# A perceiver block on one core: the dense softmax moved to the head of the following step

## The chip, the core and the metric

The kernel runs on one core of a Trainium2 chip. Its engines are TensorE (PE: matrix products and transposes, into PSUM), VectorE (DVE), ScalarE (ACT), GpSimd (POOL) and SyncE (SP, which only issues transfers); each runs its own list of instructions in order, and they wait for one another through semaphores. Sixteen DMA engines move data between HBM and the on-chip memory SBUF; SP and ACT issue to them. The metric is the device time of one execution in microseconds (us), lower is better, as the median of several executions.

## The reference

Sixteen sequences of 64 queries (width 512) attend to 16 long sequences of 1601 keys (width 384). Three blocks follow one another, each on a layer norm of the running x, and each adds to x:

```python
x = x + cross_attention(layernorm(x), ctx)   # one head of 512: softmax(q k / sqrt(512)) v, then Wo
x = x + attention(layernorm(x))              # 16 heads of 32, 64 positions; clip(q k / sqrt(32)) + q . rel[i - j],
                                             # softmax, divided once more by (its sum + 1e-8), then Wo
x = x + ffn(layernorm(x))                    # gelu(x W1 + b1) W2 + b2 with W1, W2 rounded to -1, 0, 1 by a threshold
```

## The kernel before, in words

Two sequences make a pair, 128 rows of x, so there are 8 pairs (tiles). A step n works on three of them at once: pair p = n in the cross attention, tile t = n - 1 in the first half of the dense attention, tile r = n - 2 in what is left of it. Steps 0 to 7 run; then the last two tiles finish, and the feed-forward part runs over 32 hidden blocks (2 halves of x by 16 blocks of 128 hidden units). Each engine's list is written out by hand in its own `step(n)`; all waits are semaphores.

Cross attention of pair p. PE turns the inverse deviations of the keys into rows (`key_factors`, L756), DVE multiplies the raw scores with them and finds the maximum (`scale_scores`, L1204; `exp_bias`, L1210 to 1215), ACT takes exponents in three parts (`exps`, L530), PE turns them by groups (`turn_probs`, L858), DVE scales them (`pt_scale`, L1222), and PE multiplies them with the keys as they lie (`weighted`, L871). ACT scales the context (`context_scale`, L536), PE turns it (`turn_context`, L903), and after `cT_out` (L541) `xattn_o` (L916) makes the output. DVE adds it to x and takes the moments (`x1_sum`, L1285), POOL makes the inverse deviation (`row_rstd`, L399), DVE normalises (`x1_norm`, L1294), PE turns the result (`y_turn`, L952). In the same step the next pair is prepared: statistics of its keys on DVE (`key_stats`, L1166), a power on POOL (`rstd`, L394), its x turned (`x_turn`, L723), the row that meets the keys (`a_rows`, L733), an offset (`key_offsets` on POOL, L381; `key_offset_sums` on ACT, L508), and the raw scores in four chunks (`scores`, L780) in the order 0, 1, tail, 2. The key tiles come twice: as they lie (`load_nat`, L265) and turned (`load_kt`, L278), the turned chunks through two buffers.

Dense attention of tile t. `q_rows` (L791), which opens PE's step, and `k_rows` (L802); `relative` (L833) for the relative part. A row of the relative part has to be shifted by its position: ACT copies it to SBUF (`g_out`, L567), stores it to HBM (`skew_store`, L572) and loads it back with a slanted pattern (`skew_load`, L580). `att_scores` (L844) and `clip` (DVE, L1237) make the other part, POOL adds the two (`radd`, L405), DVE subtracts the row maximum (`row_shift`, L1243 and L1245), ACT takes exponents (`row_exp`, L585), DVE makes the factors (`row_scale`, L1250 to 1260), POOL multiplies (`probs_scale`, L410), PE turns the probabilities (`att_turn`, L944). All of that is in step n = t + 1. In the next step come `att_values` (L816), `ctx_out` (L560), `att_o` (L896), `x2_sum` (L1302), `x2_norm` (L1310) and `z_turn` (L928); `values` and `v_out` (L885, L1268) make the values of tile t.

What sets the order around the change is each engine's hand-written list. POOL's in a step: x_norm, x_bias, radd(t), row_rstd(r), add_fb2(r), rstd(p+1, first half), key_offsets, probs_scale(t), rstd(p+1, second half), row_rstd(p), add_abo(p). DVE runs the statistics of the next pair's seven key groups in between: clip(t) after group 0, x2_sum(r) after 1, x2_norm(r) after 2, row_shift(t) and v_out(t) after 3, row_scale(t) after 4, and x1_sum, z_low, x1_norm after 6. The weights' magnitudes for the rounding are summed on ACT in steps 1 to 6 (`magnitude`, L608), six a step, each with a load of its own on SP.

Feed-forward. From step 7 on POOL compares the weights with the lower threshold (`neg`, L429) and DVE makes -1, 0, 1 (`ternary`, L1347). For hidden block i: PE `hidden` (L1088), ACT `gelu` (L703), DVE the high half (`gh`, L1441) and the low half (`gl`, L1443) in fp16, PE `ffn_out` (L1103) two blocks later. The softmax of the last tile is put in between at fixed blocks.

At the start PE makes a product of the two cross weights (L711), and in step 0 a product of the values' weights (`value_product`, L990), their mean (`value_mean`, L999, then `value_center` on DVE, L1363) and a bias row (`value_bias`, L1006).

Of the kernel before, what the change touches and what calls it, by code (L numbers as in the profile page):

```python
# [11 lines left out]
P = 128  # L12
# [4 lines left out]
def build_program(nc, A, out):  # L17
# [25 lines left out]
    with ctx:  # L43
# [71 lines left out]
        yTx, at = carve(at, [P, KD, P])  # L115
        a_sb, at = carve(at, [P, KC, P])
        cT, at = carve(at, [P, KC, P])
        cnat, at = carve(at, [P, DC])
# [6 lines left out]
        ssb, _ = carve(GS_AT, [P, H, L])  # L125
        psb = ssb
        b1row, _ = carve(GS_AT, [P, D])
# [27 lines left out]
        at += (NT - 2) * 4 * KD * P  # L155
        pT = []
        for _ in range(2):
            v, at = carve(at, [P, 4, P])
            pT.append(v)
# [33 lines left out]
        def sm(a, n=1):  # L193
# [9 lines left out]
                 "rel_loaded dense_loaded abv_loaded kt_tail_loaded skew_stored skew_loaded stored").split()  # L203
# [40 lines left out]

        def group(g):

            return (4, P) if g < 3 else (1, TAIL)
# [10 lines left out]
        def _(sp):  # L258
# [10 lines left out]
            def load_kt(p, ch):  # L269
# [5 lines left out]
                i = NCH * p + ch  # L275
                if i >= 2:
                    sp.wait_ge(s["chunk_scored"], 4 * ((i - 2) // NCH) + PLACE[(i - 2) % NCH] + 1)
# [31 lines left out]
            load_kt(0, NCH)  # L309
            sp.dma_start(wvT, A["wvT"]).then_inc(s["wvo_loaded"], 16)  # L310
            sp.dma_start(wo, A["wo"]).then_inc(s["wvo_loaded"], 16)
            load_kt(0, 2)
# [3 lines left out]
            load_kt(1, 0)  # L316
            load_kt(1, NCH)
            load_kt(1, 1)
# [6 lines left out]
            def step(n):  # L325
                wms, following = magnitudes(n), magnitudes(n + 1)
                more = n + 1 < NT
                for k in range(NG + 1):
# [4 lines left out]
                if n == 0:  # L333
                    sp.wait_ge(s["vbias_ps"], 1)
                    for i in range(1, 4):
                        sp.dma_start(aw[i], A["aw"][i]).then_inc(s["dense_loaded"], 16)
                if n + 2 < NT:
                    load_x(n + 2)
                if more:
                    load_kt(n + 1, 2)  # L340
                if len(wms) > 5:
                    load_wm(wms[5])
                if n + 2 < NT:
                    load_kt(n + 2, 0)
                    load_kt(n + 2, NCH)
                    load_kt(n + 2, 1)
# [14 lines left out]
        def _(pool):  # L361
# [74 lines left out]
            def step(n):  # L436
                p, t, r = stages(n)
                more = p + 1 < NT
                if more:
                    x_norm(p + 1)  # L440
                    if n == 0:
# [3 lines left out]
                        x_bias(0)  # L445
                    x_bias(p + 1)
# [3 lines left out]
                if t is not None:  # L450
                    radd(t)
# [9 lines left out]
                if t is not None:  # L461
                    probs_scale(t)
                if more:
                    rstd(p + 1, 1)
                row_rstd(p, "ln1_var", "ln1_rstd", VE1, RS1)
                add_abo(p)

# [3 lines left out]
            neg(6)  # L471
            row_rstd(LAST_T - 1, "ln2_var", "ln2_rstd", VE2, RS2)
            add_fb2(LAST_T - 1)
            neg(7)
# [10 lines left out]
        def _(act):  # L485
# [70 lines left out]
            def ctx_out(r):  # L556

                act.wait_ge(s["values_ps"], r + 1)
                for o, src in enumerate((W[1], U)):
                    act.copy(ctxT.rearrange("p (c o) r -> p o c r", o=2)[:, o, :, :], src[:, 0:2 * P].rearrange("p (c r) -> p c r", r=P)).then_inc(s["values_taken"], 1)  # L560

            def g_out(t):

                act.wait_ge(s["relative_ps"], t + 1)
                at_least(act, s["probs_turned"], 2 * t)
# [21 lines left out]
            def probs_out(t):  # L587

                at_least(act, s["values_ps"], t)
                for i, src in enumerate((W[0], W[1]) if t < LAST_T else (W[1], U)):  # L590
# [35 lines left out]
            def step(n):  # L626
                p, t, r = stages(n)
                wms = magnitudes(n)
                more = p + 1 < NT
                exps(p)  # L630
                if n == 0:
                    for m in range(KC):
                        act.wait_ge(s["xvo_ps"], m + 1)
                        act.copy(xwvo[:, m, :], S[m]).then_inc(s["xvo_taken"], 1)
                if t is not None:
                    q_out(t)
# [3 lines left out]
                if r is not None:  # L640
                    ctx_out(r)
                for i in wms[0:2]:
                    magnitude(i)
                if t is not None:
                    skew_load(t)
                context_scale(p)
                if more:
                    yTx_out(p + 1)
                if n == 0:
                    act.wait_ge(s["vbias_ps"], 1)  # L650
# [878 lines left out]
```

## Time and profile before

| | us |
|---|---|
| median of 3 runs | 689.96 |
| lowest, highest | 682.02, 702.35 |
| the profiled execution | 693.69 |
| its span, first to last instruction | 692.0 |
| PE, DVE, POOL, ACT busy in it | 556.3, 343.2, 202.1, 189.9 |

The profile is of one execution on the chip. Times in its rows count from the span's start. An engine name with q is its queue of issues; "granted clock" is the share of full speed at which TensorE's clock was let through; "idle before" is the time in which the engine stood before the instruction, with what released it. In shapes and names, `area` is the one large SBUF tensor that holds all buffers, `s_ps`, `u_ps` and `w_ps` are PSUM.

### The profile page before, as it was taken

What the parts mean: (1) busy time and instruction counts of PE and PEld (TensorE: products, weight loads), DVE (VectorE), ACT (ScalarE), POOL (GpSimd) and SP (SyncE); (2) the same over time, 40 slices, a digit from 0 to 9 for tenths busy, and PEclk for the clock granted to TensorE, in tenths of its full rate; (3) what the DMA queues carried; (4) which work ended last, traced back from release to release, by engine and by line L of the source; (5) the groups of instructions that cost most, each with busy time, mean ns of one, the idle gap of its engine ahead of it and who ended that gap; (6) DMA issues with size and microseconds to landing.
All of it is one profiled execution on the core that took longest, in us unless ns stands there. A gap on an engine that the chain in (4) does not pass through costs nothing.

```text
span 692.0 us, 10456 instructions
## 1 busy us (share of the span) xinstructions
PE 556.3 (80%) x4171; PEld 318.4 (46%) x4171; DVE 343.2 (50%) x769; ACT 189.9 (27%) x447; POOL 202.1 (29%) x136
## 2 busy tenths in 40 slices
PE   3979989907894989589678949896892878899997
PEld 1834455505452745365254517453641733344443
DVE  5814644453267237435732582284348178955333
ACT  0232124122413422341224124322401323121111
POOL 0131242042225204320522251043347376710000
PEclk9889999967998899799989988997996899999999
DMA  8975995925485387449544953760432242001001
GB/s 320 391 295 202 349 371 200 325 74 198 144 300 210 123 262 265 139 169 340 166 185 143 309 209 122 218 238 31 169 91 91 93 92 91 31 1 53 9 1 62
DMA packets 41617, 122.46 MB, mean 177 GB/s; under 512 B 19544, under 2 KB 21336, under 8 KB 36704
## 3 DMA queue, kind: packets, MB, share of 16 engines
q1 hardware_dynamic: 23776, 109.20, 43.5%
q10 hardware_dynamic: 17792, 12.58, 7.1%
q8 instruction: 33, 0.54, 0.3%
q14 instruction: 16, 0.13, 0.1%
HBM read 111.29 MB, written 10.49 MB: 176 GB/s over the span
## 4 chain that ended last, share of the span: by engine, by line
PE 42%; DMA 20%; DVE 12%; POOL 12%; ACT 7%; issue 6%; ACTq 1%; SPq 0%; DVEq 0%; POOLq 0%
DMA area<-skew 13%; PE s_ps L1103 7%; PE w_ps L1088 6%; PE s_ps L780 5%; PE u_ps L791 4%; PE u_ps L871 4%; POOL area L394 4%; DVE area L1166 4%; DMA skew<-area 3%; POOL area L429 3%; ACT area L567 2%; POOL area L405 2%; DMA area<-in_kt_dram 2%; PE s_ps L711 2%; PE w_ps L896 2%
## 5 line engine op out<-in xcount | busy, mean ns | idle before, releaser
L1166 DVE BATCH_NORM_STATS2 area<-area 128x6 f32<-128x384 f32 (+1 forms) x208 | 99.3, 544 | 3.9 <-DMA area<-in_nat_dram 3.9
L780 PE MATMUL s_ps<-area 128*64 128x512 f32 (+1 forms) x384 | 79.5, 560 | 5.8 <-DMA area<-in_kt_dram 4.7
L871 PE MATMUL u_ps<-area 128*64 128x384 f32 (+1 forms) x416 | 81.9, 543 | 0.3 <-DVE area L1222 0.3
L1103 PE MATMUL s_ps<-area 128*128 128x512 f16 x256 | 61.0, 381 | 8.6 <-DVE area L1443 8.6
L952 PE MATMUL w_ps<-area 128*128 128x128 f32 x32 | 8.5, 415 | 72.5 <-DVE area L1294 72.5
L1222 DVE TENSOR_TENSOR area<-w_ps,area 128x512 f32<-128x512 f32 (+1 forms) x32 | 18.8, 591 | 90.3 <-PE w_ps L858 90.3
L429 POOL TENSOR_SCALAR area<-area 128x512 f16<-128x512 f32 x32 | 54.9, 1730 | 28.1 <-DVE area L1334 14.3
L1088 PE MATMUL w_ps<-area 128*128 128x512 f16 x256 | 61.7, 383 | 0.1
L405 POOL TENSOR_TENSOR area<-area 128x1024 f32<-128x1024 f32 x8 | 18.8, 2354 | 145.6 <-DMA area<-skew 145.6
L1204 DVE CUSTOM_DVE_ANT_0 area<-w_ps,area 128x512 f32<-128x512 f32 x24 | 15.3, 689 | 89.6 <-PE w_ps L756 89.6
L780 PEld LDWEIGHTS s_ps<-area 128*64 128x64 f32 x384 | 25.9, 150 | 51.2 <-issue 48.9
L871 PEld LDWEIGHTS u_ps<-area 128*64 128x64 f32 (+1 forms) x416 | 30.6, 150 | 38.9 <-issue 37.3
L703 ACT ACTIVATE area<-w_ps,area 128x512 f32<-128x512 f32 x32 | 21.9, 687 | 88.8 <-PE w_ps L1088 74.3
L394 POOL TENSOR_TENSOR area<-area 128x16 f32<-128x16 f32 (+1 forms) x16 | 39.0, 2440 | 17.5 <-DVE area L1181 17.5
L1103 PEld LDWEIGHTS s_ps<-area 128*128 128x128 f16 x256 | 24.4, 97 | 40.6 <-DVE area L1443 10.8
L952 PEld LDWEIGHTS w_ps<-area 128*128 128x128 f32 x32 | 5.4, 207 | 73.7 <-DVE area L1294 73.7
L1088 PEld LDWEIGHTS w_ps<-area 128*128 128x128 f16 x256 | 24.6, 97 | 31.8 <-issue 3.0
L1441 DVE TENSOR_SCALAR area<-area 128x512 f16<-128x512 f32 x32 | 17.5, 547 | 43.3 <-ACT area L703 43.3
L1347 DVE SCALAR_TENSOR_TENSOR area<-area 128x512 f16<-128x512 f32 x32 | 31.1, 1014 | 14.4 <-POOL area L429 11.2
L371 POOL TENSOR_TENSOR area<-area 128x1 f32<-128x1 f32 x8 | 4.9, 610 | 112.4 <-DVE area L1154 112.4
L896 PE MATMUL w_ps<-area 128*128 128x512 f32 x64 | 31.1, 629 | 2.4 <-ACT area L560 2.4
L791 PEld LDWEIGHTS u_ps<-area 128*128 128x128 f32 x256 | 30.3, 197 | 5.7 <-issue 5.7
(167 smaller groups left out, 901.7 us busy)
## 6 DMA issues: line engine op xcount, KB each, us to landing
area<-in_nat_dram SPq DMA_DIRECT2D x48, 768.0 KB, 9.8
area<-in_kt_dram SPq DMA_DIRECT2D x24, 1536.0 KB, 6.7
area<-in_wf_dram SPq DMA_DIRECT2D x32, 256.0 KB, 7.2
skew<-area ACTq DMA_DIRECT2D x8, 1024.0 KB, 3.9
area<-in_wf_dram SPq DMA_DIRECT2D x16, 512.0 KB, 3.3
area<-in_aw_dram SPq DMA_DIRECT2D x4, 1024.0 KB, 7.8
area<-skew ACTq DMA_DIRECT2D x16, 256.0 KB, 6.8
area<-in_x_dram SPq DMA_DIRECT2D x8, 256.0 KB, 10.4
```

The costliest lines, as they stand in the source:

```text
L394: pool.tensor_tensor(rs[p % 2][:, sl], ve[:, sl], minus_half[:, 0:sl.stop - sl.start], ALU.pow).then_inc(s["rs_ready"], 1)
L405: pool.tensor_tensor(ssb, ssb, rsk, ALU.add).then_inc(s["radd_done"], 1)
L429: pool.tensor_scalar(wneg[f % 2][:, w, :], wraw[f % 4][:, w, :], sm(WNTHR + w), None, ALU.is_lt).then_inc(s["neg_done"], 1)
L703: act.activation(gf[i % 2], HID[i % 2][:, :], ACT.Gelu, bias=col("ffn_b1", i % KF), scale=1.0).then_inc(s["gelu_done"], 1)
L780: ins = pe.matmul(S[ch][u * L:(u + 1) * L, 0:n], a_sb[:, c, u * L:(u + 1) * L], x[:, u, c, :], start=(c == 0), stop=(c == KC - 1))
L791: ins = pe.matmul(U[:, m * P:(m + 1) * P], awq[:, c, m * P:(m + 1) * P], yT[:, c, :], start=(c == 0), stop=(c == KD - 1))
L871: ins = pe.matmul(U[u * L:(u + 1) * L, 0:DC], pT[g % 2][0:m, i, u * L:(u + 1) * L], nat[0:m, j, u, :], start=(j == 0), stop=(j == NJ - 1))
L896: ins = pe.matmul(dst[:, :], ctxT[:, c, :], awo[:, c, :], start=(c == 0), stop=(c == KD - 1))
L1088: ins = pe.matmul(HID[i % 2][:, :], wf16[:, f, 0, c * P:(c + 1) * P], zt[:, 4 * h:4 * h + 4, z, c, :], start=(k == 0), stop=(k == 2 * KD - 1))
L1103: ins = pe.matmul(S[q], g[i % 3][:, q * P:(q + 1) * P], wf16[:, f, 1, :], start=(f == 0 and z == 0), stop=(f == KF - 1 and z == 1))
L1166: dve.bn_stats(st[b][0:m, 2 * j + u, :], nat[0:m, j, u, :]).then_inc(s["key_stats"], 1)
L1347: dve.scalar_tensor_tensor(out=wf16[:, f, w, :], in0=wraw[f % 4][:, w, :], scalar=sm(WTHR + w), in1=wneg[f % 2][:, w, :], op0=ALU.is_gt, o ...
```

## The change

The dense softmax of a tile is taken apart. The skew load is issued later in ACT's step (after cT_out), radd becomes the last of POOL's step, and row_shift, row_exp, row_scale, probs_scale and att_turn run in the next step, on tile r: row_shift behind exp_bias, row_scale behind pt_scale(0), att_turn behind the last `weighted`. q_out goes ahead of the exponents on ACT; ctx_out and the copies of the probabilities behind context_scale. On PE, x_turn goes behind turn_context, att_values behind att_scores. clip no longer waits for the store. Among the buffers, ssb gets a place of its own, a_sb and yTx lie inside gs, and cnat and cT inside the two pT buffers.

Pairs 0 and 1 get a buffer of their own (kt_first) for their third turned key chunk. Its loads are issued ahead of wvT and wo (pair 0) and once pair 0 is scored (pair 1). wqT is loaded ahead of x(0). value_bias runs right behind value_product, and with it the three dense weight loads go ahead of pair 1's key tiles on SP. In the feed-forward part the high half of the gelu is made on ACT, right behind the gelu, with the wait for its buffer; DVE keeps the low half. Core of the diff:

```diff
+        RING = [(p, ch) for p in range(NT) for ch in range(NCH) if p > 1 or ch < 2]
+        SLOT = {k: i for i, k in enumerate(RING)}
...
+                if (p, ch) not in SLOT:
+                    at_least(sp, s["chunk_scored"], 4 * p)
+                    sp.dma_start(kt_first, A["kt"][p, ch]).then_inc(s["kt_first_loaded"], 16)
+                    return
...
+            sp.dma_start(wqT, A["wqT"]).then_inc(s["wq_loaded"], 16)
             load_x(0)
-            sp.dma_start(wqT, A["wqT"]).then_inc(s["wq_loaded"], 16)
...
             def step(n):          # SP
+                if n == 0:
+                    sp.wait_ge(s["vbias_ps"], 1)
+                    for i in range(1, 4):
+                        sp.dma_start(aw[i], A["aw"][i]).then_inc(s["dense_loaded"], 16)
                 for k in range(NG + 1):
                     if more:
                         load_nat(n + 1, k)
...
             def step(n):          # POOL
+                if r is not None:
+                    probs_scale(r)
                 if more:
                     x_bias(p + 1)
...
-                if t is not None:
-                    radd(t)
                 if r is not None:
                     row_rstd(r, "ln2_var", "ln2_rstd", VE2, RS2)
                     add_fb2(r)
                 if more:
                     rstd(p + 1, 0)
                     key_offsets(p + 1)
+                    rstd(p + 1, 1)
...
                 row_rstd(p, "ln1_var", "ln1_rstd", VE1, RS1)
                 add_abo(p)
+                if t is not None:
+                    radd(t)
...
             def step(n):          # ACT, after the change
                 if t is not None:
                     q_out(t)
                 exps(p)
...
                 if r is not None:
                     row_exp(r)
                 if t is not None:
                     k_out(t)
                     g_out(t)
                     skew_store(t)
                 for i in wms[0:2]:
                     magnitude(i)
                 context_scale(p)
                 if r is not None:
                     probs_out(r)
                     ctx_out(r)
                 cT_out(p)
                 if t is not None:
                     skew_load(t)
                 if more:
                     yTx_out(p + 1)
...
             for i in range(2 * KF):   # ACT, feed-forward
                 act.activation(gf[i % 2], HID[i % 2][:, :], ACT.Gelu, bias=col("ffn_b1", i % KF), scale=1.0).then_inc(s["gelu_done"], 1)
+                act.wait_ge(s["gelu_done"], i + 1)
+                if i >= 3:
+                    h, f = (i - 3) // KF, (i - 3) % KF
+                    if f < KF - 1:
+                        act.wait_ge(s["ffn_step"], (KF - 1) * h + f + 1)
+                    else:
+                        act.wait_ge(s["ffn_out_ps"], 4 * (h + 1))
+                act.activation(gh[i % 3], gf[i % 2], ACT.Identity, bias=0.0, scale=sm(FS)).then_inc(s["gelu_high"], 1)
...
                 weighted(p, 3)        # PE, after the change
                 if r is not None:
                     att_turn(r)
                 if t is not None:
                     att_scores(t)
                 if n == 0:
                     value_mean()
                 if r is not None:
                     att_values(r)
                 turn_context(p)
                 if more:
                     x_turn(p + 1)
                 if r is not None:
                     att_o(r)
                 if more:
                     a_rows(p + 1)
...
                 exp_bias(p)           # DVE, after the change
                 if n == 0:
                     value_dots()
                 if r is not None:
                     row_shift(r)
                 if n == LAST_T:
                     small_values()
                 if more:
                     x_stats(p + 1)
                 pt_scale(p, 0)
                 if r is not None:
                     row_scale(r)
                 pt_scale(p, 1)
...
             def parts(i):         # DVE, feed-forward
-                dve.tensor_scalar(gh[i % 3], gf[i % 2], sm(FS), None, ALU.mult).then_inc(s["gelu_high"], 1)
                 dve.wait_ge(s["gelu_high"], i + 1)
```

Behind step 7 the same order holds for the last two tiles: POOL runs neg(5), neg(6), probs_scale(6), neg(7), row_rstd(6), add_fb2(6), radd(7); PE runs q_rows, k_rows and relative of tile 7, then att_turn(6), att_scores(7), att_values(6), att_o(6), values(7); DVE row_shift(6), ternary(5), row_scale(6), ternary(6), clip(7), x2_sum(6), ternary(7), x2_norm(6), v_out(7).

## Rows read from the trace of the kernel before

**Rows 1.** List of waits, whole span: engine, line, waited for: us in total, times, longest.
```profile
POOL area L405 <- DMA area<-skew: 145.6, 6, 32.1
...
PE w_ps L952 <- DVE area L1294: 72.5, 8, 22.4
...
PE w_ps L858 <- ACT area L560: 13.5, 6, 2.3
```

**Rows 2.** Chain that ended last, in order of time: start us, us, what.
```profile
98.43 3.77 PE u_ps L791 x32
...
291.85 3.77 PE u_ps L791 x32
...
310.14 18.83 DMA area<-skew
329.11 2.35 POOL area L405
...
356.85 3.77 PE u_ps L791 x32
...
482.32 3.77 PE u_ps L791 x32
```

**Rows 3.** PE timeline, step 4: start us, us, engine, line, op, out<-in, count [idle before <-releaser].
```profile
307.08 4.49 PE L871 MATMUL u_ps<-area 128*64 128x384 f32 x16
...
312.09 2.80 PE L871 MATMUL u_ps<-area 128*64 128x384 f32 x16
...
318.45 0.66 PE L723 MATMUL w_ps<-area 128*128 128x128 f32 x4
...
350.50 1.11 PE L952 MATMUL w_ps<-area 128*128 128x128 f32 x4 [7.11 <-DVE area L1294]
```

**Rows 4.** Windows: us, busy PE, PEld, DVE, ACT, POOL (instructions), PE clock, DMA share, GB/s.
```profile
52.50:103.50 51.00, 47.77 (x238) 24.78 (x237) 25.98 (x72) 12.05 (x28) 14.32 (x10) 1.00 0.81 308
...
296.50:361.50 65.00, 51.76 (x445) 31.24 (x444) 30.79 (x76) 20.95 (x54) 17.89 (x12) 0.89 0.60 205
...
591.00:638.00 47.00, 46.98 (x271) 21.38 (x272) 29.27 (x43) 9.87 (x16) 11.93 (x8) 1.00 0.03 10
```

**Rows 5.** DVE timeline, step 4, end of exp_bias.
```profile
298.70 0.21 DVE L1215 TENSOR_SCALAR area<-area 128x1 f32<-128x1 f32 x1
```

**Rows 6.** Groups by line and shape: count | busy us, mean ns | idle before.
```profile
L1441 DVE TENSOR_SCALAR area<-area 128x512 f16<-128x512 f32 x32 | 17.5, 547 | 43.3 <-ACT area L703 43.3
...
L1245 DVE TENSOR_TENSOR area<-area 128x1024 f32<-128x1024 f32 x8 | 9.8, 1225 | 0.3
...
L508 ACT ACTIVATE area<-area 128x512 f32<-128x512 f32 x8 | 5.0, 630 | 76.4 <-POOL area L381 76.4
...
L703 ACT ACT_TABLE_LOAD x2 | 2.6, 1283 | 4.3 <-issue 4.3
...
L394 POOL TENSOR_TENSOR area<-area 128x16 f32<-128x16 f32 x8 | 23.4, 2920 | 7.0 <-DVE area L1181 7.0
```

**Rows 7.** Page, DMA issues: count, KB each, median us from issue to landing.
```profile
area<-in_kt_dram SPq DMA_DIRECT2D x24, 1536.0 KB, 6.7
...
skew<-area ACTq DMA_DIRECT2D x8, 1024.0 KB, 3.9
```

**Rows 8.** Loads of the skewed scores (L580), time from issue to landing.
```profile
DMA to landing us min/median/max: 4.0/6.8/21.6
```

**Rows 9.** Timelines of PE and DVE, start and step 0.
```profile
45.17 5.39 PE L780 MATMUL s_ps<-area 128*64 128x512 f32 x12 [3.85 <-DMA area<-in_kt_dram]
...
77.03 2.07 DVE L1363 SCALAR_TENSOR_TENSOR area<-area,s_ps 128x512 f32<-128x512 f32 x3 [4.42 <-PE s_ps L999]
```

**Rows 10.** PE timeline, step 7, y_turn.
```profile
534.53 1.11 PE L952 MATMUL w_ps<-area 128*128 128x128 f32 x4 [10.23 <-DVE area L1294]
```

**Rows 11.** Chain in order of time, feed-forward.
```profile
591.02 1.90 PE s_ps L1103 x8
592.92 1.74 PE w_ps L1088 x8
```

More of the change, by code:

```diff
@@ L124, in build_program @@
         gs, at = carve(at, [P, H, REL])
-        ssb, _ = carve(GS_AT, [P, H, L])
+        ssb, at = carve(at, [P, H, L])
         psb = ssb
+        a_sb, _ = carve(GS_AT, [P, KC, P])
+        yTx, _ = carve(GS_AT + 6144, [P, KD, P])
         b1row, _ = carve(GS_AT, [P, D])
@@ L332, in step @@
                         load_wm(wms[(1, 3, NG).index(k) + 2])
[L333 to L336, printed above, removed]
                 if n + 2 < NT:
                     load_x(n + 2)
-                if more:
+                if more and n:
                     load_kt(n + 1, 2)
@@ L471, in _ @@
             neg(6)
+            probs_scale(LAST_T - 1)
+            neg(7)
             row_rstd(LAST_T - 1, "ln2_var", "ln2_rstd", VE2, RS2)
             add_fb2(LAST_T - 1)
-            neg(7)
             radd(LAST_T)
@@ L629, in step @@
                 more = p + 1 < NT
+                if t is not None:
+                    q_out(t)
                 exps(p)
@@ L1034, in step @@
                 weighted(p, 3)
-                if more:
-                    x_turn(p + 1)
+                if r is not None:
+                    att_turn(r)
                 if t is not None:
@@ L1040, in step @@
                     value_mean()
-                    value_bias()
+                if r is not None:
+                    att_values(r)
+                turn_context(p)
+                if more:
+                    x_turn(p + 1)
                 if r is not None:
                     att_o(r)
-                turn_context(p)
                 if more:
@@ L1067, in _ @@
             relative(LAST_T)
+            att_turn(LAST_T - 1)
+            att_scores(LAST_T)
             att_values(LAST_T - 1)
@@ L1392, in step @@
                     ternary(0)
-                    ternary(1)
+                stats(1)
                 if t is not None:
                     clip(t)
-                stats(1)
+                if not more:
+                    ternary(1)
+                stats(2)
                 if r is not None:
                     x2_sum(r)
-                stats(2)
-                if r is not None:
-                    x2_norm(r)
                 if not more:
@@ L1404, in step @@
                 stats(3)
+                if r is not None:
+                    x2_norm(r)
+                stats(4)
                 if t is not None:
-                    row_shift(t)
                     v_out(t)
-                stats(4)
                 if not more:
                     ternary(3)
-                if t is not None:
-                    row_scale(t)
                 stats(5)
```

140 lines of the change are left out of this document (69 added, 71 removed).

## The prediction

> **What bounds the kernel now.** I read the page's busy shares first, which show no engine full, TensorE (PE) ahead of VectorE (DVE), GpSimd (POOL) and ScalarE (ACT). Then the list of waits: the longest is POOL's radd (L405) waiting for the load of the skewed relative scores, 145.6 us in 6 waits; on PE the largest is y_turn (L952) waiting for x1_norm (L1294), 72.5 us in 8 [rows 1]. The chain in order of time joins the two. In step 4 (q_rows starts at 291.85, that of step 5 at 356.85, a step of 65.0 us) the load runs from 310.14 to 329, then radd, and from there POOL and DVE work off in order what stood behind it [rows 2]: row_rstd and add_fb2, rstd(p+1), the row softmax, the last key statistics, x1_sum and x1_norm. PE's timeline shows the end of that: it idles 7.11 us before y_turn [rows 3]. And each pause slows what follows: weighted(0), after a pause, takes 4.49 us for the same 16 matmuls that take 2.80 at 312.09 [rows 3]. The stretch of step 4 has PE busy 51.76 of 65.0 us at a mean granted clock of 0.89 (a mix of its two levels, 1.2 and 2.4 GHz), DVE 30.8, ACT 21.0, POOL 17.9, and DMA at a share of 0.60 [rows 4]. So steps 1 to 6, from 98.43 to 482.32 [rows 2], 383.9 us of the 692.0 span, are bound by one transfer's latency and what is queued behind it. The feed-forward part at the end is another regime: PE busy 46.98 of 47.0 us at clock 1.00 [rows 4].
>
> **The change, part by part.**
>
> *The softmax moved.* radd(t) now stands last in POOL's step, behind rstd, key_offsets, row_rstd(p) and add_abo(p); the reductions, the exponent and the scaling follow in the next step. No arithmetic is removed; an order is. With nobody waiting for the skew load inside the step, PE's own work is the next bound: 51.76 us x 0.89 = 46.1 us per step if the clock stays at its upper level. (That treats all busy time as scaling with the clock; the 4.49/2.80 pair says a little less, so 46 to 47.)
>
> Where the moved work lands, counting from T, the start of q_rows. DVE's head: exp_bias ends at T+7.1 as now (its last row at 298.70 [rows 5]), row_shift takes two passes of 1.23 us [rows 6], x_stats 1, so pt_scale(0) ends at about T+11.3, and weighted(0) starts then. PE reaches it at about T+10.7, because relative no longer waits for q_out behind the exponents (about a microsecond) and turn_probs(1) no longer for ctx_out (L858's 13.5 us in 6 [rows 1] go). So the head costs PE about 0.6 us, and it saves those two waits. row_scale (one pass of 1.2 like row_shift's and five short ones; I put 2.4 us) sits before pt_scale(1) and is over before weighted(0) is. probs_scale on POOL ends near T+16; att_turn needs it at T+21. Its cover is weighted(0); if the row exponent came 2 us late, PE would lose those 2 us.
>
> The middle. x_turn started 26.6 us after q_rows in step 4 (318.45 [rows 3]); without the two waits (about 3.4 together) and the slow weighted(0) (1.7) all keys are weighted at T+21, and att_turn, att_scores, att_values and turn_context go to T+24. The skew load, now behind cT_out on ACT, is issued at about T+25. What is queued behind its wait for the store is yTx_out, and a_rows on PE behind that; the store is issued at T+14 and took 3.9 us (median of 8 [rows 7]), so the wait costs nothing up to a store of 10 us. a_sb and yTx now share memory with gs, which this same wait guards. The new waits on PE (att_turn for probs_scale, x_turn and att_values for probs_out, key_factors for the tile before's z_low) end earlier than PE arrives; the tightest is probs_out, at T+22.8, just when att_values is due, and behind it stand turn_context, x_turn and att_o. clip's wait for the store goes; it never came last. Behind att_o runs a chain over four engines, with the lengths of step 4: att_o ends at T+28; x2_sum with its moments 1.8, stats(3) with the variance 2.5, x2_norm 0.6: T+32.9; on POOL add_fb2 1.3, rstd 2.9 [rows 6], key_offsets 1.3: T+38.4; on ACT key_offset_sums, scores_out, a magnitude, two spreads and z_out 4.1: T+42.5; z_low and x1_norm 1.2: T+43.7. PE, with values, scores(0), xattn_o, z_turn and two more chunks, is there at T+43.3: another 0.5 us lost.
>
> The end. The third key chunk of the next pair still waits for the first to be scored (T+37) and must land before scores(2) at T+44: 6.7 us in the median [rows 7] against 7. That is the tightest place; a landing of 8 us costs 1 us per step.
>
> radd itself then starts at about T+45 and must be over at the next step's T+7, that is 55 us after T; the load has 48.5 + 7 - 2.4 - 25 = 28 us to land. radd itself is 2.4 [rows 2]. The longest landing that the trace shows is 21.6 [rows 8], with the key tiles in flight beside it. So it is covered.
>
> How much above 46.1? From below 46.1 plus the 0.6 and some 0.5 at y_turn: 47.2. From above, step 0: the same loop without dense softmax kept PE busy 47.77 of 51.0 us at clock 1.00 [rows 4], that is 94%; 46.1/0.94 = 49.0. I take 48.5, nearer to the measured row than to my addition. Step 1 has no att_turn, att_values, att_o and z_turn of an earlier tile, about 5 us less: 43.5. Sum of the six: 43.5 + 5 x 48.5 = 286.0, against 383.9: **98 us less**. Bounds: 46.1 a step (110 less) and 53 a step, a DMA-like bound below (75 less).
>
> *Own buffer for the third chunk of pairs 0 and 1, and the start.* PE waits 3.85 us for pair 0's third chunk until 45.17, and its 12 matmuls then take 5.39 us [rows 9], at the lower clock level; half of it at the upper. So some 6.5 us vanish there. What is late next: x(1)'s load, queued behind all of pair 1's chunks, then the three dense weight loads (3 MB), now in front of pair 1's key tiles on SP, since SP waits for value_bias first: by the chunk's row (1.5 MB in 6.7 us [rows 7]) at most 13 us of transfer. DVE's value_center, which ends at 79.1 [rows 9], comes about 3.5 us earlier; the key statistics behind it run without a break to x1_sum. value_bias moved ahead is the same PE work. The wqT load ahead of x(0) (256 KB) gives under a microsecond. I take **4.4 us** for step 1's start; bounds 0 (the key tiles land late) and 8.
>
> *The turn to the feed-forward.* In step 7 the softmax leaves POOL's row of threshold passes (neg) and DVE's of ternary; y_turn, now at 534.53 after 10.23 us of idle PE [rows 10], comes about 4.5 us earlier from the step's start. Against it, probs_scale(5) now stands ahead of the first neg, and the softmax of tile 6 comes back between q_rows(7) and att_turn(6), a wait of about 3 us. Later POOL's wait for the last row_scale shrinks, as DVE has less in front of it. The fifth second-layer group starts at 591.02 [rows 11], 108.7 us after step 7 began; from there on PE is full. I add up 101: **7.5 us less**. Bounds 0 and 12.
>
> *The gelu's high part on ACT.* 32 DVE passes of 547 ns leave DVE, and ACT gets 32 of about 630 ns (the nearest row, an Identity over 512 columns [rows 6]). Per hidden block ACT then has two such passes, 1.3 us, and PE two groups of 1.74 [rows 11], 3.5; PE is full there [rows 4], so **0** in the steady part; what is gained sits in the 7.5. Its new wait (the third last block's second layer) stands ahead of the next gelu on ACT, but PE runs that layer before the hidden block in question. The Trainium skill, "ScalarE: Activation LUTs", section "Rules for kernel authors", speaks against the move: multiplications belong on VectorE. The rows agree in direction, 630 against 547 ns; by the rule alone each block's latency grows 0.08 us, which the full PE hides, so the sum is the same by both.
>
> Sum: 693.7 (span 692.0 and 1.7 around it) - 98 - 4.4 - 7.5 = **584 us**. The profiled execution lies 0.5% above the median of the three shown (689.96); their spread, 682 to 702, is mostly, I suppose, the skew load's, which no longer counts, so I don't correct for it.
>
> **Rivals.** (1) *The stall passes to the next chain*: the third chunk lands late or x1_norm does, a step takes 52 to 54. For: the slack is under 1 us in both places, and the DMA share of 0.60 x 65 = 39 us per step fills 80% of 48.5. Against: most transfers are issued well before their use. 5 x 3.5 to 5.5 more: 602 to 612. (2) *ACT swaps function tables* between Gelu and Identity in every block. A table load is 1.28 us [rows 6]; two per block make ACT 1.3 + 2.6 = 3.9 us against PE's 3.5, 32 x 0.4 = 13 more: 597. No row shows an Identity after a Gelu. Against: in the steps Identity runs between Exps without a load, and there are two loads in all ahead of 32 Gelus [rows 6] though copies run between them. The same page of the Trainium skill, section "Table sets: the hidden batching unit", says that identity is in every set, by which this rival is nil. (3) *The change doesn't free the chain*: the load lands 30 to 40 us after issue since it now meets the key chunks; radd, then row_shift in front of pt_scale, hold PE. 6 x (2 to 12) more: 596 to 656. (4) *Slower*: the same wait at the head, but beyond a landing of 28 + 16 = 44 us a step is longer than 65 us; at 48 us it is 68.5, and the time 584 + 6 x 20 = 704. For: every step must now pass it before its first weighted key. Against: twice the longest landing [rows 8].
>
> **How the numbers follow.** Forecast 0.66, (1) 0.22, (2) 0.04, (3) 0.06, (4) 0.02. The forecast's own range is 566 to 601. To 8 in 10 with the bounds (all lower bounds together 564, steps of 53 give about 610, and 619 with nothing at start and end) I take 567 to 620. A measurement of this kernel tells about 2% from no change; faster by over 2%: 0.96, within 2%: 0.02, slower: 0.02.
>
> **What would show it.** Right: radd waits no longer for the load, or only at a step's end; steps of 47 to 50 us with granted clock about 1.00; PE's pauses before y_turn under 1 us; q_rows of step 7 near 380; the feed-forward's steady part unchanged. Wrong: pauses of several us before scores(2) (rival 1), table loads inside the feed-forward (2), row_shift waiting for radd (3, 4).

## The result, and the profile after

The changed kernel takes **587.61 us** (median of 4 runs, 586.64 to 589.15) against 696.13 us of the kernel before, run beside it (4 runs, 682.02 to 702.35). The ratio is **0.8568**, 95% interval 0.8478 to 0.8658; like all ratios below it leaves out runs more than 1.5% above the fastest of their kernel, so here it goes by 682.02 and 689.96. The forecast was 584, in a range of 567 to 620. The profiled execution took 587.82 us, with a span of 586.1.

The chain of waits of the changed kernel, in order of time (start us, us, what), answers to [rows 2]. q_rows, which opens a step, is now L818, the key chunks' scores L807, weighted L897, y_turn L978, radd L419:

```profile
40.99 17.86 DMA area<-in_x_dram
...
96.70 3.77 PE u_ps L818 x32
...
129.94 9.90 DMA area<-in_kt_dram
139.88 4.33 PE s_ps L807 x12
144.21 3.77 PE u_ps L818 x32
...
191.02 3.77 PE u_ps L818 x32
...
238.76 3.77 PE u_ps L818 x32
...
286.53 3.77 PE u_ps L818 x32
...
335.36 3.77 PE u_ps L818 x32
...
381.86 3.77 PE u_ps L818 x32
```

The skew load is gone from the chain. Steps 1 to 6 take 47.5, 46.8, 47.7, 47.8, 48.8 and 46.5 us, 285.2 in all. The windows (us; PE, PEld, DVE, ACT, POOL busy; PE clock; DMA share; GB/s) are of step 1, step 3, step 5, the turn, and the feed-forward, to be read beside [rows 4]:

```profile
96.70:144.20 47.50, 42.38 (x362) 25.69 (x360) 23.69 (x61) 16.73 (x44) 13.94 (x9) 0.96 0.71 236
...
191.00:238.80 47.80, 46.59 (x446) 28.92 (x445) 31.13 (x75) 21.04 (x54) 17.93 (x13) 1.00 0.83 278
...
286.50:335.40 48.90, 46.73 (x446) 29.07 (x445) 31.16 (x75) 21.03 (x54) 17.69 (x12) 1.00 0.82 265
...
381.90:483.20 101.30, 80.04 (x744) 49.85 (x744) 56.77 (x102) 34.55 (x66) 60.62 (x37) 0.92 0.36 110
483.20:586.10 102.90, 98.80 (x500) 43.61 (x500) 37.57 (x49) 37.99 (x55) 12.07 (x9) 0.98 0.07 26
```

From step 2 on PE is the bound: 46.59 of 47.80 us at the upper clock level. Before, the same matmuls kept PE busy for 51.76 us in step 4, at a mean clock of 0.89 [rows 4]. PE's two pauses per step, in the timeline of step 5 (answering [rows 3]), have shrunk to almost nothing, and weighted(0) takes 2.80 us:

```profile
297.67 2.80 PE L897 MATMUL u_ps<-area 128*64 128x384 f32 x16 [0.18 <-DVE area L1250]
...
331.97 0.66 PE L978 MATMUL w_ps<-area 128*128 128x128 f32 x4 [0.23 <-DVE area L1321]
```

The view of the skew load's line (L594) shows who waited for it, and its landings; [rows 1] had 145.6 us here. What is left is one wait of radd, at the end of step 1:

```profile
  POOL area L419: 3.0, 1
...
DMA to landing us min/median/max: 4.2/12.7/22.6
```

The store, the load and the key chunks have themselves become slower, not faster. The page's issues (count, KB, median us to landing), against [rows 7, 8]:

```profile
area<-in_kt_dram SPq DMA_DIRECT2D x24, 1536.0 KB, 8.0
skew<-area ACTq DMA_DIRECT2D x8, 1024.0 KB, 8.6
```

Store 3.9 to 8.6, load 6.8 to 12.7, key chunk 6.7 to 8.0. What was won is cover, not speed.

In the turn to the feed-forward, PE's timeline shows what is left:

```profile
427.89 1.11 PE L978 MATMUL w_ps<-area 128*128 128x128 f32 x4 [9.12 <-DVE area L1321]
...
442.21 1.09 PE L970 MATMUL w_ps<-area 128*128 128x128 f32 x8 [2.38 <-POOL area L424]
...
483.24 2.56 PE L1131 MATMUL s_ps<-area 128*128 128x512 f16 x8 [3.22 <-DVE area L1466]
485.59 2.97 PE L1116 MATMUL w_ps<-area 128*128 128x512 f16 x8
```

Apart from the wait for the first weights (10.3 us at the very start), the largest pause of PE is now y_turn's in step 7, 9.12 us.

### The profile page after: what moved, and what is told of

It is laid out like the page before. It is cut to its first block, busy times and chain, and to the rows that moved or that the text cites. A ratio compares the mean times of both kernels' runs of the same rounds, so it can differ in the third digit from the quotient of the medians.

```text
span 586.1 us, 10422 instructions
## 1 busy us (share of the span) xinstructions
PE 531.4 (91%) x4171; PEld 305.2 (52%) x4171; DVE 324.8 (55%) x737; ACT 213.9 (36%) x479; POOL 200.7 (34%) x136
## 4 chain that ended last, share of the span: by engine, by line
PE 60%; DVE 11%; POOL 9%; issue 9%; DMA 7%; ACT 3%; SPq 0%; DVEq 0%; ACTq 0%; POOLq 0%
PE u_ps L897 12%; PE s_ps L1131 8%; PE w_ps L1116 7%; PE s_ps L807 7%; PE w_ps L920 5%; PE u_ps L818 5%; POOL area L443 4%; DMA area<-in_kt_dram 3%; DMA area<-in_x_dram 3%; PE w_ps L757 2%; PE s_ps L734 2%; PE w_ps L911 2%; POOL area L408 2%; DVE area L1194 2%; PE w_ps L885 1%
## 5 line engine op out<-in xcount | busy, mean ns | idle before, releaser
L897 PE MATMUL u_ps<-area 128*64 128x384 f32 (+1 forms) x416 | 74.1, 500 | 4.8 <-DVE area L1250 4.8
L807 PE MATMUL s_ps<-area 128*64 128x512 f32 (+1 forms) x384 | 72.2, 519 | 3.4 <-DMA area<-in_kt_dram 2.3
L1466 DVE SCALAR_TENSOR_TENSOR area<-area 128x512 f16<-128x512 f32 x32 | 27.0, 844 | 58.3 <-ACT area L726 58.1
L443 POOL TENSOR_SCALAR area<-area 128x512 f16<-128x512 f32 x32 | 53.4, 1684 | 2.1 <-DVE area L1374 2.1
L897 PEld LDWEIGHTS u_ps<-area 128*64 128x64 f32 (+1 forms) x416 | 28.1, 138 | 38.8 <-issue 30.7
L807 PEld LDWEIGHTS s_ps<-area 128*64 128x64 f32 x384 | 24.1, 140 | 43.3 <-issue 37.9
L413 POOL TENSOR_TENSOR area<-area 128x1 f32<-128x1 f32 x16 | 9.8, 613 | 93.1 <-DVE area L1305 93.1
L385 POOL TENSOR_TENSOR area<-area 128x1 f32<-128x1 f32 x8 | 4.9, 612 | 101.2 <-DVE area L1182 101.2
L1374 DVE SCALAR_TENSOR_TENSOR area<-area 128x512 f16<-128x512 f32 x32 | 28.0, 916 | 19.5 <-POOL area L443 16.3
L818 PEld LDWEIGHTS u_ps<-area 128*128 128x128 f32 x256 | 30.8, 200 | 6.8 <-issue 5.7
L818 PE MATMUL u_ps<-area 128*128 128x128 f32 x256 | 32.3, 286 | 0.7 <-ACT area L617 0.7
L829 PE MATMUL w_ps<-area 128*128 128x128 f32 x256 | 30.5, 277 | 0.0
## 6 DMA issues: line engine op xcount, KB each, us to landing
area<-skew ACTq DMA_DIRECT2D x16, 256.0 KB, 12.7
area<-in_x_dram SPq DMA_DIRECT2D x8, 256.0 KB, 10.7
```

Source lines behind the costliest of these rows:

```text
L443: pool.tensor_scalar(wneg[f % 2][:, w, :], wraw[f % 4][:, w, :], sm(WNTHR + w), None, ALU.is_lt).then_inc(s["neg_done"], 1)
L807: ins = pe.matmul(S[ch][u * L:(u + 1) * L, 0:n], a_sb[:, c, u * L:(u + 1) * L], x[:, u, c, :], start=(c == 0), stop=(c == KC - 1))
L818: ins = pe.matmul(U[:, m * P:(m + 1) * P], awq[:, c, m * P:(m + 1) * P], yT[:, c, :], start=(c == 0), stop=(c == KD - 1))
L829: ins = pe.matmul(W[0][:, m * P:(m + 1) * P], awk[:, c, m * P:(m + 1) * P], yT[:, c, :], start=(c == 0), stop=(c == KD - 1))
L897: ins = pe.matmul(U[u * L:(u + 1) * L, 0:DC], pT[g % 2][0:m, i, u * L:(u + 1) * L], nat[0:m, j, u, :], start=(j == 0), stop=(j == NJ - 1))
L1374: dve.scalar_tensor_tensor(out=wf16[:, f, w, :], in0=wraw[f % 4][:, w, :], scalar=sm(WTHR + w), in1=wneg[f % 2][:, w, :], op0=ALU.is_gt, o ...
```

## Experiments

Three questions: was it the transfer's latency, or the order of the work behind it, that cost the time; what were the smaller parts worth; and can what is left be had? Step means below are over steps 2 to 6, from PE's starts of q_rows: 63.2 us before (166.17 to 482.32), 47.5 after (144.21 to 381.86).

**No round trip, changed kernel.** For t > 0 the store and the load of the skewed scores are left out, and radd waits for the first load only, so that later tiles add the first one's values. `skew_load`, for one:

```diff
+                if t:
+                    return
```

> The changed kernel with the skew store and load of the dense rows left out for every row after the first (rows 1 to 7 then add the first row's values, so their relative scores are not computed); everything else as it is. Theory (the round trip lies wholly beside other work in the six steps): 584 to 588 us, steps of 46.5 to 48 us as in the changed kernel, at most 1 us a step from transfers of the other loads that land sooner. Rival (the round trip still holds the steps or the turn): 560 to 578 us, with the gain in the steps or between the last step's start and the fifth output group.

587.25 us (583.71 to 589.82; ratio to before 0.8556, 0.8453 to 0.8658). Steps of 47.6 in the mean (145.04 to 383.21). In the changed kernel the trip is hidden in steps and turn: its time, steps and turn are the changed kernel's within what single executions differ.

**No round trip, kernel before.** The same in the kernel before, where clip waits for the first store only as well.

> The kernel before, with the same store and load left out for rows 1 to 7 (the same part is not computed). Theory (the round trip is part of the lost time, and the rest is the order: the softmax of a row in the same step stands on POOL and DVE ahead of the next pair's normalisation, and the turning pauses lower the clock): POOL's add can start at the end of the clip, 7.9 us sooner in the step that starts at 291.85, and the step's pauses shrink but don't vanish: 52 to 55 us a step, 615 to 632 us. Rival A (the round trip is all of it): steps near the changed kernel's 47.5, 590 to 600 us. Rival B (the trip was hidden before too, and it is the order alone): 680 to 692 us.

671.32 us (666.9 to 672.8; ratio 0.9774, 0.9681 to 0.9867): none of the three, and nearest to rival B. By the ratio, taking the transfer away saves some 15 us (9 to 22 by the interval), where theory wanted 615 to 632 us and rival A 590 to 600; the steps still take 59.8 us (162.35 to 461.46). PE's pause is still there, and so is the lowered clock, 0.91 over the step from 281.8 to 342.0 (list of waits, then PE's timeline of the step that starts at 281.81):

```profile
POOL area L405 <- DVE area L1240: 83.6, 5, 16.7
...
PE w_ps L955 <- DVE area L1297: 66.8, 8, 22.2
```

```profile
335.28 1.12 PE L955 MATMUL w_ps<-area 128*128 128x128 f32 x4 [6.66 <-DVE area L1297]
...
338.03 4.04 PE L783 MATMUL s_ps<-area 128*64 128x512 f32 x12
```

radd (L405) no longer waits for the load, but it waits for the clip, 83.6 us in 5 times, and what is queued behind it on POOL waits too. The chain of that step shows the rest:

```profile
317.35 1.86 DVE area L1169 x4
319.99 2.92 POOL area L394
322.91 1.25 POOL area L381
324.18 0.73 ACT area L508 x2
325.23 0.96 ACT area L588
326.21 1.23 DVE area L1253
328.56 2.85 DVE area L1169 x6
332.17 1.96 POOL area L394
334.13 0.52 POOL area L399
334.68 0.56 DVE area L1297
335.28 1.12 PE w_ps L955 x4
```

It crosses four engines and comes back: key statistics (DVE), their inverse deviations and the offsets (POOL), the offsets' sums and behind them the dense row's exponent (ACT, L588), the row's scaling and behind it the last statistics (DVE), and again POOL and DVE before y_turn. The dense softmax and the next pair's normalisation are threaded into one chain because each engine's list interleaves them. That interleaving is what the change undid.

**One instruction back.** In POOL's list of the changed kernel:

```diff
+                if t is not None:
+                    radd(t)
                 if r is not None:
                     row_rstd(r, "ln2_var", "ln2_rstd", VE2, RS2)
...
                 add_abo(p)
-                if t is not None:
-                    radd(t)
```

> The changed kernel with one instruction put back on POOL: the addition of the skewed scores stands ahead of the second layer norm's reciprocal root and the key factors again, instead of at the end of the step; DVE, ACT, PE and the transfers keep the changed order. Theory (what the change took away is POOL's queue behind a transfer): POOL stands at the addition until the load has landed, some T+37 to T+41 of the step, and the key factors, key offsets and first layer norm behind it come 8 to 12 us later; steps of 55 to 59 us, 632 to 655 us in all. Rival (the softmax's place on DVE, ACT and PE is what counts, POOL's queue place is free): 586 to 592 us.

643.12 us (639.39 to 645.7; ratio 0.9367, 0.9243 to 0.9492): as theory said. Steps of 56.7 (151.12 to 434.49), so that in the new order radd's place in POOL's queue is worth 9.1 us a step. POOL's timeline, then PE's, then the chain:

```profile
305.58 2.34 POOL L419 TENSOR_TENSOR area<-area 128x1024 f32<-128x1024 f32 x1 [22.85 <-DMA area<-skew]
```

```profile
311.61 1.09 PE L952 MATMUL w_ps<-area 128*128 128x128 f32 x4 [6.26 <-DVE area L1295]
...
319.43 0.66 PE L978 MATMUL w_ps<-area 128*128 128x128 f32 x4 [2.75 <-DVE area L1321]
```

```profile
290.44 15.01 DMA area<-skew
```

So radd's old place puts the load back on the chain, and the 9.1 us hold both: the clip it also needs ended at 291.68, 13.9 us before radd began. What the early place would cost without the load was not tried. The remaining 6.5 us (63.2 to 56.7, single executions) are put down by difference to the rest of the new order, on DVE, ACT and PE.

**The load late.** In ACT's step the skew load goes to the end; the wait for the store stays where it stood:

```diff
                 if t is not None:
-                    skew_load(t)
+                    act.wait_ge(s["skew_stored"], 16 * (t + 1))
...
                 for i in wms[4:6]:
                     magnitude(i)
+                if t is not None:
+                    skew_load(t)
```

> The changed kernel with the skew load issued at the end of ACT's step, some 20 us later (ACT waits for the store to have landed where the load stood, since the turned x overwrites the stored tile). Theory (the load has about 15 us of slack: it may be issued until about T+39 with a landing of 12.7 us, and POOL's addition must end by T+54.7, where DVE's row maximum takes it): issued at about T+45 it lands at the next step's T+10, the row maximum starts about 5 us late, and PE's first weighted sum with it: steps of 51 to 54 us from step 2 on, 610 to 630 us. Rival (the trip has no part in the time any more, its wait is covered wherever it is issued): 586 to 592 us.

655.19 us (653.4 to 658.1; ratio 0.9553, 0.9479 to 0.9628): the place is the one that theory named, the size twice what it said, 59.2 us a step. In the step that starts at 313.13, POOL's and DVE's timelines, and PE's:

```profile
327.08 2.34 POOL L419 TENSOR_TENSOR area<-area 128x1024 f32<-128x1024 f32 x1 [15.97 <-DMA area<-skew]
```

```profile
329.45 1.22 DVE L1272 TENSOR_REDUCE area<-area 128x16 f32<-128x1024 f32 x1 [9.19 <-POOL area L419]
```

```profile
333.62 4.52 PE L899 MATMUL u_ps<-area 128*64 128x384 f32 x16 [9.46 <-DVE area L1252]
```

The load was issued at 313.58 and 314.50, after the next step's q_rows had begun and not 3 us ahead of it: ACT's last work of a step, the copy of the fourth chunk's scores, lies there. The second half landed after 12.45 us, PE lost 9.46, and the matmuls behind the pause ran at the lower level (4.52 for 2.80). So the slack is real but finite: issued at T+24.2 (step 2), as the change has it, nobody waits from step 2 on; issued just behind the step's end, a step is 11.7 us longer.

**The gelu's high part back on DVE.**

```diff
+                dve.tensor_scalar(gh[i % 3], gf[i % 2], sm(FS), None, ALU.mult).then_inc(s["gelu_high"], 1)
...
-                act.activation(gh[i % 3], gf[i % 2], ACT.Identity, bias=0.0, scale=sm(FS)).then_inc(s["gelu_high"], 1)
```

> The changed kernel with the high part of the gelu back on DVE (one multiplication by the scale per half block, with the waits it had), nothing else undone. Theory (in the steady part of the feed-forward both engines lie beside PE, so the move is worth nothing there and at most the first blocks of the turn): 587 to 591 us, the half blocks still 1.73 and 1.74 us apart on PE. Rival (the move carries the 5.5 us that the turn and the feed-forward gained): 592 to 595 us.

585.55 us (584.01 to 587.96; ratio 0.8531, 0.849 to 0.8572). Not slower, and below both expectations: the move is worth nothing that shows, and the pair at the end of this section says so again. In the window from 500 to 560 PE is full either way, here with DVE at 24.90 and ACT at 12.29 us, in the changed kernel (second row) with 17.76 and 24.87:

```profile
500.00:560.00 60.00, 60.00 (x280) 26.78 (x279) 24.90 (x40) 12.29 (x18) 0.04 (x1) 1.00 0.05 18
```

```profile
500.00:560.00 60.00, 59.95 (x279) 26.58 (x277) 17.76 (x24) 24.87 (x36) 1.85 (x2) 1.00 0.05 18
```

**No third buffer.**

```diff
-        RING = [(p, ch) for p in range(NT) for ch in range(NCH) if p > 1 or ch < 2]
+        RING = [(p, ch) for p in range(NT) for ch in range(NCH)]
```

with the old order of the key chunks on SP.

> The changed kernel without the third key buffer: all chunks go through the ring of two again, in the old order of SP's list, also in the first step; the later dense weights, the first x and everything of the steps stay changed. Theory (the third buffer lets pair 0 be scored without a pause, and x(1), which SP issues behind the last of pair 0, hangs on that): pair 0 is scored 4 to 6 us later, and x(1), the first weighted sum and the whole rest with it: 591 to 595 us. Rival (the start is set by the key statistics of pair 1, whatever the buffer does): 586 to 589 us.

589.92 us (585.73 to 594.36; ratio 0.8589, 0.853 to 0.8648), and in its profile step 1 starts at 99.81, 3.1 us later than in the changed kernel's and 1.6 later than in the latest of the seven profiles with that kernel's start (95.57 to 98.22). The pause before pair 0's third chunk is back (4.27 us, and 4.15 for its matmuls), but what followed was no longer x(1): the chain goes through the loads and statistics of pair 1's keys. That both had a part is the reading of this one profile; the time, 589.92, lies between its two expectations and decides nothing.

**x(1) early.**

```diff
+            load_x(1)
             load_kt(1, 0)
...
-            load_x(1)
```

> The changed kernel with the load of x(1) put ahead of the first key chunk of pair 1 in SP's list, so that it is not held behind the chunk that waits for pair 0 to be scored. Theory (what took back 2.7 of the 4.4 us expected of the start is this load, issued at 40.99 and landed after 17.86): the first step ends 3 to 5 us sooner, 582 to 585 us. Rival (behind x(1) stands the next thing, the key statistics and their loads): 586 to 588 us.

583.88 us (581.09 to 586.25; ratio 0.8503, 0.8454 to 0.8552). Step 1 starts at 93.96, 2.7 us sooner than in the changed kernel's profile; in the four profiles with this load early it starts at 93.85 to 94.20, below all seven without. The times alone don't show it: the nearest kernel run on the same chip, with the gelu's high part on DVE, took 585.55, and the intervals overlap. PE's pause before weighted(0), 3.92 us in the changed kernel, is 0.35; y_turn's is now 4.11, behind key statistics whose loads land late:

```profile
59.16 10.47 DMA area<-in_nat_dram
...
69.65 1.94 DVE area L1194 x4
```

**Third buffer for pair 2 too**, in addition:

```diff
-        RING = [(p, ch) for p in range(NT) for ch in range(NCH) if p > 1 or ch < 2]
+        RING = [(p, ch) for p in range(NT) for ch in range(NCH) if p > 2 or ch < 2]
...
+                if n == 1:
+                    load_kt(2, 2)
...
-                if more and n:
+                if more and n > 1:
```

> As the run before, and the third chunk of pair 2 also goes to the third buffer, loaded at the head of SP's list for step 1 instead of behind that step's key rows and x. Theory (step 1 took 47.5 instead of 43.5 us because its third chunk landed 9.90 us after the buffer came free): step 1 of 43.5 to 45 us, 579 to 582 us in all. Rival (the rest of step 1 is later too, or the next pair's chunks pay): within 1 us of the run before.

579.23 us (577.96 to 579.68; ratio 0.8434, 0.8396 to 0.8472). Step 1 takes 42.7 us (94.20 to 136.93); its last chunk's matmuls take 2.80 us and don't wait. All six executions lie below the lowest of the run before.

**The turn, and all together.** POOL's and DVE's lists of step 7 and behind it:

```diff
-                else:
-                    neg(3)
-                    neg(4)
                 row_rstd(p, "ln1_var", "ln1_rstd", VE1, RS1)
...
+            neg(3)
+            neg(4)
+            probs_scale(LAST_T - 1)
             neg(5)
             neg(6)
-            probs_scale(LAST_T - 1)
...
             row_shift(LAST_T - 1)
-            ternary(5)
+            ternary(3)
             row_scale(LAST_T - 1)
-            ternary(6)
+            ternary(4)
             clip(LAST_T)
+            ternary(5)
+            ternary(6)
```

(ternary(3) and ternary(4) leave DVE's step.) Four kernels on one chip:

> The changed kernel once more, as the measure for the other three runs beside it: 586 to 589 us.

> The changed kernel with two half blocks of the weights' ternary form (the comparison on POOL and its partner on DVE, blocks 3 and 4) moved out of the last step, behind the last first layer norm and row 6's softmax; row 6's scaling of the probabilities goes ahead of blocks 5 and 6 on POOL. Theory (in the last step y_turn waits 9.12 us for a normalisation that stands behind these on DVE and POOL, and this pause, not the dense chain, is what the turn still loses): y_turn 6 us sooner, the turning of row 6's probabilities up to 8 us sooner, 579 to 582 us. Rival (the ternary blocks themselves are the turn's bound, so that what is won ahead is lost at the first hidden blocks): 586 to 589 us.

> All three together: x(1) early, the third buffer for pair 2 also, and the turn's blocks moved. If the gains are in different stretches they add up: 588 less 3 (start) less 4 to 5 (step 1) less 6 to 9 (turn), 571 to 575 us. If the turn's blocks are the bound: 578 to 581 us.

> The same with the high part of the gelu back on DVE. Theory (the move is worth nothing to within a microsecond or two, either way): within 2 us of the run before. Rival (with ternary blocks later, DVE has more to do beside the first hidden blocks, so that the extra pass shows): 3 to 6 us over it.

| | median us | lowest, highest | ratio to before, interval |
|---|---|---|---|
| changed kernel | 585.07 | 581.51, 588.55 | 0.8543, 0.8485 to 0.8602 |
| turn | 578.84 | 576.13, 580.48 | 0.8446, 0.8403 to 0.8489 |
| all three | 573.84 | 571.45, 576.0 | 0.8373, 0.8327 to 0.842 |
| all three, gelu's high part on DVE | 573.47 | 571.4, 575.3 | 0.8375, 0.834 to 0.8411 |

The measure itself came out at 585.07, a little below what was expected of it. Against it the turn gives 6.2 us. In its profile the fifth second-layer group starts 93.8 us after step 7 began (379.56 to 473.31) instead of 101.4:

```profile
419.31 0.66 PE L977 MATMUL w_ps<-area 128*128 128x128 f32 x4 [2.76 <-DVE area L1320]
...
473.31 1.90 PE L1130 MATMUL s_ps<-area 128*128 128x512 f16 x8 [3.21 <-DVE area L1463]
```

y_turn waits 2.76 us for 9.12. All three together give 11.2 us and lie in the expected 571 to 575. The last pair of rows, 573.84 and 573.47, is the gelu's move once more: nil.

## Why the prediction was right, and where its steps were off

**What bounds the kernel before.** "Bound by one transfer's latency and what is queued behind it" was right, but neither half has a price of its own. In the old order, taking the transfer away is worth 3.4 us of a step (63.2 to 59.8), and rather less, since the profile of the kernel before is one of its longer executions (693.69); then the chain through the softmax holds the step. In the new order radd's early place costs 9.1, with the load back on the chain. The parts are not independent, so the 15.7 us of a step can't be divided between them. The total didn't suffer, because it was built up from PE's work at the full clock and not from the wait that would vanish: 693.7 less the 145.6 us of waits for the load would have been 548, below the range.

**The six steps**: 286.0 predicted, 285.2 measured, but as two errors that cancel. Steps 2 to 6 were put at 48.5 each and took 47.5: the bound from step 0's 94% was the wrong neighbour, and the addition (46.1 for PE, 0.6 and 0.5 for two pauses, 47.2) was nearer. PE's floor measured 46.3 to 46.7 at clock 1.00, which bears out 51.76 x 0.89. The pauses were smaller than worked out, 0.18 and 0.23 in step 5. Step 1 was put at 43.5 and took 47.5, because its third chunk landed 9.90 us after its issue and held PE at 139.88, where scores then ran at the lower level; with the chunk in the third buffer it takes 42.7.

**The tight place** was rightly named and rightly sized. A landing of 8 us was to cost 1 us. The median over all key chunks did become 8.0, but the third chunks of steps 1 to 6 landed in 9.9, 7.1, 6.8, 8.0, 6.8 and 6.4 us: that of step 4, at 8.0, cost PE 0.89 us (283.73), and apart from step 1's no other cost anything. The median of all chunks wasn't that of the chunk that counts.

**The skew load** is issued at T+24.2 (predicted T+25), lands in 12.7 in the median, 22.6 at most (the prediction had a cover of 28), and radd waits for it once, 3.0 us at the end of step 1. Rival 3 had its place right, as the late load shows, and not its condition.

**The start**: 4.4 predicted, 1.7 measured, from one profile to the other. That difference isn't clear of what executions differ by: in the kernel before without the round trip, whose step 0 is unchanged, step 1 starts at 95.03 and not 98.43, and in the seven profiles with the changed kernel's start at 95.57 to 98.22. What the term left out is sure: in "what is late next" x(1)'s load was named and given no price. SP issues it behind the chunk that waits for pair 0 to be scored, it lands 17.86 us later, and weighted(0) waits 3.92 us (3.40 to 3.92 in six of the seven, 0.66 in one) and then takes 4.50 us for 2.80. Put ahead, it gives back 2.7.

**The turn**: 7.5 predicted, 5.5 measured, from the starts of step 7 to the end (209.7 before, 204.2 after). The 101 us up to the fifth second-layer group came out at 101.4. What came out longer is the stretch behind it, 102.9 for 101.0: behind a pause of 3.22 us the first groups took 2.56 and 2.97 us. When the changed kernel was profiled again, a pause of 3.21 us stood there too, the groups took 1.90 us, that stretch 101.2 and the whole turn 201.3, 8.4 less than before. So 7.5 lies between two executions.

**The gelu's move**: 0 predicted, 0 found. ACT's pass was put at 630 ns and took 724, with PE full over both. Rival 2 is out; the groups by line:

```profile
L726 ACT ACTIVATE area<-area 128x512 f16<-128x512 f32 x32 | 23.2, 724 | 1.0
...
L718 ACT ACT_TABLE_LOAD x2 | 2.6, 1283 | 2.3 <-issue 2.3
```

32 Identity passes lie between 32 Gelus with the same two loads as before [rows 6]. The Trainium skill, "ScalarE: Activation LUTs", section "Table sets: the hidden batching unit", says that identity is in every set, and the trace agrees for the Gelu's.

Sum: 693.7 - 98.7 - 1.7 - 5.5 = 587.8, the profiled execution's 587.82. That the spread of the kernel before is the skew load's, as the prediction supposes, isn't shown: without the round trip its four runs spread by 5.9 us, but with the addition early and with the load late, where radd waits for the load, they spread by 6.3 and 4.7.

## What to carry to other kernels

When a long wait heads the list, ask what stands behind the waiting instruction on its engine before asking how to shorten the wait: here one addition at its old place in POOL's list cost the new order 55 us (643.12 against 587.61), while removing the transfer that it waits for gained the old order some 15. Forecast such a change from what bounds next (busy time at the full clock, plus the pauses that a step-by-step schedule leaves), not from the sum of the waits. And when a load moves in a queue, price what stands behind every waiting entry: both misses of this forecast, x(1) and the third chunk of pair 2, were loads held behind a wait for a buffer, and the second then landed late.

## What was not expected

Some transfers got slower in the new order: the medians to landing rose by a fifth (key chunks) to twofold (store and load), while the DMA share rose from 0.60 to 0.83 in a step; the key tiles as they lie stayed at 9.8 us. The shorter steps alone don't explain it: with radd early, in steps of 56.7 us, the store and the load took 8.7 and 12.7 us as well. The skew load takes part in the others' slowness. Step 1's third chunk landed in 9.1 to 9.9 us in five profiles in which it was issued with that load in flight (9.90 in the changed kernel, the load issued from 118.7 on), and in 6.9 in the kernel with the load late. And without the round trip the third chunks of steps 2 to 6 landed in 6.2 to 6.7 us, against 6.4 to 8.0, x in 7.6 against 10.7, and by the page's issues:

```profile
area<-in_nat_dram SPq DMA_DIRECT2D x48, 768.0 KB, 8.1
area<-in_kt_dram SPq DMA_DIRECT2D x24, 1536.0 KB, 7.8
```

That is 8.1 for 9.8 for the key tiles as they lie, but only 7.8 for 8.0 for all key chunks. The Trainium skill, "Trainium Kernel Development and Optimization", section "Key Constraints", says that transfers issued from different engines' queues run on the same 16 DMA engines and interleave, which these landings agree with. Why step 1's third chunk suffers most stays open.

In one place of the changed kernel PE pauses for nothing that the profile shows, 1.76 us in step 5, after 61 of the 64 small matmuls of `att_values` (L845). A pause on that line stands once in each of the twelve profiles with the new order, 1.3 to 1.9 us in eleven and 0.2 in one, and in neither with the old. In the profile of all three together it is 1.78 us and the granted clock of that stretch falls to 0.83, so that the step takes 50.4 us instead of 48.8; in the changed kernel the matmuls behind it kept their speed. What it is stays open.
